# Making keys and values per node instead of per gathered edge row in a four-layer graph network

## The reference

```python
K = (x @ Wk.T + bk).reshape(N, HEADS, HEAD_DIM)
V = (x @ Wv.T + bv).reshape(N, HEADS, HEAD_DIM)
Q = x.reshape(N, HEADS, HEAD_DIM)
scores = jnp.sum(K[src] * Q[dst], axis=-1) / np.sqrt(HEAD_DIM)
m = jax.ops.segment_max(scores, dst, num_segments=N)
e = jnp.exp(scores - m[dst])
attn = e / (jax.ops.segment_sum(e, dst, num_segments=N)[dst] + 1e-16)
out = jax.ops.segment_sum(V[src] * attn[:, :, None], dst, num_segments=N)
return out.reshape(N, DIM_H) @ Wo.T + bo
```

## Time and profile before

| | |
|---|---|
| median of 3 runs | 6019.27 us (6014.14 to 6030.68) |
| the profiled execution | 6022.17 us |
| its span in the trace | 6020.4 us |
| its mean granted clock of TensorE | 0.809 of 2.4 GHz |
| busy, share of the span | PE 63%, DVE 66%, ACT 34%, POOL 50% |
| moved from and to HBM | 995 MB, 165 GB/s |

### The profile page before, as it was taken

The page is one execution under the profiler, slowest core; times in us unless marked ns, Lnnn a source line. Parts: engine busy times, 40 slices in busy tenths (PEclk is TensorE's granted clock), DMA queues, the critical chain, the costliest instruction groups (busy, mean ns, idle before and its releaser), DMA issues. The chain is left out here.

```text
span 6020.4 us, 90405 instructions
## 1 busy us (share of the span) xinstructions
PE 3782.8 (63%) x16668; PEld 2549.2 (42%) x16668; DVE 3973.2 (66%) x12622; ACT 2020.3 (34%) x4450; POOL 2987.1 (50%) x2764
## 2 busy tenths in 40 slices
PE   0688884333489985559965556776500198988940
PEld 0466653333267764444444445555400043433410
DVE  8555555888388873654455556656578798888856
ACT  0444452333122221225556542222144433333310
POOL 0644442777677600000057768777700267777730
PEclk9788886555799997989977779888855599999975
DMA  6566665777455544877777767777578511111149
GB/s 226 147 160 159 156 159 152 230 221 211 121 127 145 142 157 153 255 241 229 229 230 234 226 187 135 133 127 133 94 256 271 177 32 38 43 46 47 48 156 377
DMA packets 986437, 994.99 MB, mean 165 GB/s; under 512 B 210641, under 2 KB 648417, under 8 KB 986163
## 3 DMA queue, kind: packets, MB, share of 16 engines
q1 hardware_dynamic: 676899, 628.12, 36.1%
q0 software_dynamic: 131904, 146.31, 12.7%
q10 hardware_dynamic: 177488, 218.95, 10.3%
HBM read 560.95 MB, written 466.16 MB: 171 GB/s over the span
## 5 line engine op out<-in xcount | busy, mean ns | idle before, releaser
L703 POOL DMA_INDIRECT at_first_table<-n_h,n_first_edge x784 | 792.6, 1011 | 1280.9 <-ACT n_h L271 924.5
L2489 PE MATMUL e_m<-e_by_rel,rel_w 128*128 128x512 f32 x1568 | 727.9, 619 | 0.0
L695 POOL DMA_INDIRECT e_xs<-x_table,e_idx x392 | 376.8, 961 | 514.1 <-POOLq L2379 395.0
L695 POOL DMA_INDIRECT e_x<-x,e_idx x392 | 376.9, 961 | 447.5 <-ACT e_h L271 241.0
L695 POOL DMA_INDIRECT e_hs<-h_table,e_idx x392 | 422.3, 1077 | 172.1 <-issue 108.1
L2403 DVE SCALAR_TENSOR_TENSOR e_by_rel<-e_y,e_part_t 128x512 f32<-128x512 f32 x784 | 476.5, 681 | 33.3 <-PE e_y L2504 27.7
L703 POOL DMA_INDIRECT rel_sum_table<-e_res,e_again x392 | 393.8, 1005 | 148.8 <-issue 125.5
L2489 PEld LDWEIGHTS e_m<-e_by_rel,rel_w 128*128 128x128 f32 x1568 | 306.1, 201 | 352.8 <-issue 352.8
L1008 PE MATMUL n_m<-n_mean,n_pick 128*128 128x129 f32 x784 | 203.4, 440 | 338.7 <-DVE n_pick L1073 323.0
L2481 PE MATMUL e_t<-ident,e_part 128*128 128x128 f32 x392 | 69.1, 304 | 550.7 <-ACT e_part L271 438.7
L711 POOL DMA_INDIRECT sum_table<-e_res,e_target x196 | 308.5, 1574 | 139.5 <-issue 58.9
(11 more groups left out here) (374 smaller groups left out, 10328.1 us busy)
## 6 DMA issues: line engine op xcount, KB each, us to landing
x_table<-n_x ACTq DMA_DIRECT2D x294, 256.0 KB
n_x<-x_table SPq DMA_DIRECT2D x294, 256.0 KB
e_hd<-at_first_table SPq DMA_DIRECT2D x196, 256.0 KB
mean_runs_table<-e_packed SPq DMA_DIRECT2D x196, 130.0 KB
n_mean<-mean_runs_table SPq DMA_DIRECT2D x392, 65.0 KB
at_first_table<-prep_zero ACTq DMA_DIRECT2D x1, 25088.0 KB
e_edge<-edge128T SPq DMA_DIRECT2D x98, 256.0 KB
e_keep<-col_tab_table SPq DMA_DIRECT2D x196, 128.0 KB
```

The source lines that it names most:

```text
L695: pool.indirect_dma_start(out=tile[:, t, :], out_offset=None, in_=table, in_offset=bass.IndirectOffsetOnAxis(ap=idx[:, col + t:col + t + 1 ...
L703: pool.indirect_dma_start(out=table, out_offset=bass.IndirectOffsetOnAxis(ap=idx[:, t:t + 1], axis=0), in_=tile[:, t, :], in_offset=None, ...
L2489: ins = pe.matmul(flat(at(ps_m, u - 6)), k.rel_w[:, r, :], at(by_rel, u - 6)[:, r, :], start=(r == 0), stop=(r == RELS - 1))
```

## The change

Each node's 128 keys and 128 values (without their biases) are made in the mean node stage and stored side by side as one row of 1 KB in a new table `key_val`. There PE turns the four tiles of `h1` (four transposes), ACT copies them from PSUM to `h1t`, PE multiplies each with `wkv`, the two weight matrices side by side (four products of 256 columns), ACT copies these in two halves to `key_val` and issues the store. ACT's list grows from a lag of 5 turns to one of 10, PE's from 1 to 8. `h1` is still stored and scattered.

The edge stage gathers from `key_val`. PE turns the key half alone, DVE multiplies it straight from PSUM with the queries (the keys' bias is added there, as before) one turn earlier than before, and ACT copies the value half, from SBUF, into a ring of 30 in place of `hst`. The key product and the value product are gone from PE's list, and DVE's message product reads the copied values in SBUF. The freed PSUM banks make both turning targets double. The gather of a slot now waits for PE's turning and for ACT's copy.

```diff
@@ mean node stage, PE
+                j = i - 8
+                if live(j, S):
+                    pe.wait_ge(h1t_ready, j + 1)
+                    if begun(j - 1):
+                        pe.wait_ge(key_val_ready, j)
+                    for t in range(TILES):
+                        ins = pe.matmul(ps_kv[t // HALVES][:, t % HALVES, :], at(h1t, u)[:, t, :], k.wkv[:, :], start=True,
+                                        stop=True)
+                    ins.then_inc(key_val_done, 1)
+                j = i - 6
+                if live(j, S):
+                    pe.wait_ge(h1_ready, j + 1)
+                    if begun(j - 1):
+                        pe.wait_ge(h1t_ready, j)
+                    for t in range(TILES):
+                        ins = pe.transpose(ps_h[:, t, :], at(h1, u - 6)[:, t, :], k.ident[:, :])
+                    ins.then_inc(h1_turned, 1)
@@ mean node stage, ACT
+                        act.wait_ge(h1_turned, j - 3)
                     norm.apply(act, at(h1, u), at(x1, u), ACT.Relu, j, u).then_inc(h1_ready, 1)
...
+                j = i - 7
+                if live(j, S):
+                    act.wait_ge(h1_turned, j + 1)
+                    if begun(j - 2):
+                        act.wait_ge(key_val_done, j - 1)
+                    act.activation(at(h1t, u - 7)[:, :, :], ps_h[:, :, :], ACT.Copy).then_inc(h1t_ready, 1)
+                j = i - 9
+                if live(j, S):
+                    act.wait_ge(key_val_done, j + 1)
+                    if begun(j - 4):
+                        act.wait_ge(at(key_val_out, u - 9), moved(j - 4, u - 9))
+                    for b in range(HALVES):
+                        ins = act.activation(at(key_val, u - 9)[:, HALVES * b:HALVES * b + HALVES, :], ps_kv[b][:, :, :],
+                                             ACT.Copy)
+                    ins.then_inc(key_val_ready, 1)
+                j = i - 10
+                if live(j, S):
+                    act.wait_ge(key_val_ready, j + 1)
+                    act.dma_start(rows_of(scratch["key_val"], j), flat(at(key_val, u - 10))
+                                  ).then_inc(at(key_val_out, u - 10), 16)
+            run_steps(act, body, S, 10, 16)
@@ edge stage
-        hs, hs_in = ph.loaded("hs", [P, TILES, D])
+        hs, hs_in = ph.loaded("hs", [P, TILES, 2 * D])
-        hst, hst_ready = ph.made("hst", [D, ROWS], HELD)
+        val, val_ready = ph.made("val", [P, TILES, D], HELD)
-        ps_hs, ps_hd, ps_k, ps_v, ps_p, ps_r = (ph.ps(n) for n in ("hs", "hd", "k", "v", "p", "r"))
+        ps_hs, ps_hd, ps_p, ps_r = ph.banks("kt"), ph.banks("qt"), ph.ps("p"), ph.ps("r")
@@ edge stage, POOL
                     pool.wait_ge(hs_turned, i - 3)
+                    pool.wait_ge(val_ready, i - 3)
                 pool.sem_inc(pool_turn, 1)
-                gather(pool, at(hs, i), scratch["h1"], idx[:, i, :], 0, at(hs_in, i))
+                gather(pool, at(hs, i), scratch["key_val"], idx[:, i, :], 0, at(hs_in, i))
@@ edge stage, DVE
-                j = n - 3
+                j = n - 2
                 if 0 <= j < S:
-                    dve.wait_ge(k_done, j + 1)
+                    dve.wait_ge(hs_turned, j + 1)
...
-                    dve.scalar_tensor_tensor(at(kq, j)[:, :], flat(ps_k), k.bk[:, :], at(hdt, j)[:, :], ALU.add, ALU.mult
+                    dve.scalar_tensor_tensor(at(kq, j)[:, :], flat(at(ps_hs, j)), k.bk[:, :], at(hdt, j)[:, :], ALU.add, ALU.mult
...
-                                      ps_v[:, :, :].rearrange("p t (h c) -> p t h c", c=HEAD_DIM),
+                                      at(val, j)[:, :, :].rearrange("p t (h c) -> p t h c", c=HEAD_DIM),
@@ edge stage, ACT
-                    act.wait_ge(hs_turned, j + 1)
+                    act.wait_ge(at(hs_in, j), moved(j, j, TILES))
                     if j >= HELD:
-                        act.wait_ge(v_done, j - HELD + 1)
-                    act.activation(at(hst, j)[:, :], flat(ps_hs), ACT.Copy).then_inc(hst_ready, 1)
+                        act.wait_ge(pv_ready, j - HELD + 1)
+                    act.activation(at(val, j)[:, :, :], at(hs, j)[:, :, D:2 * D], ACT.Copy).then_inc(val_ready, 1)
@@ edge stage, PE
-                    if i:
-                        pe.wait_ge(hst_ready, i)
+                    if i >= 2:
+                        pe.wait_ge(kq_ready, i - 1)
                     for t in range(TILES):
-                        ins = pe.transpose(ps_hs[:, t, :], at(hs, i)[:, t, :], k.ident[:, :])
+                        ins = pe.transpose(at(ps_hs, i)[:, t, :], at(hs, i)[:, t, 0:D], k.ident[:, :])
                     ins.then_inc(hs_turned, 1)
-                j = n - 2
-                if 0 <= j < S:
-                    pe.wait_ge(hst_ready, j + 1)
-                    if j:
-                        pe.wait_ge(kq_ready, j)
-                    pe.matmul(flat(ps_k), k.wk[:, :], at(hst, j)[:, :], start=True, stop=True).then_inc(k_done, 1)
...
-                j = n - 29
-                if 0 <= j < S:
-                    pe.wait_ge(hst_ready, j + 1)
-                    if j:
-                        pe.wait_ge(pv_ready, j)
-                    for t in range(TILES):
-                        ins = pe.matmul(ps_v[:, t, :], at(hst, j)[:, t * P:(t + 1) * P], k.wv[:, :], start=True, stop=True)
-                    ins.then_inc(v_done, 1)
```

More of the change, by code:

```diff
@@ L285, in __init__ @@
         self.w1_edge = tile("w1_edge", [D, D])
-        self.wk = tile("wk", [D, D])
-        self.wv = tile("wv", [D, D])
+        self.wkv = tile("wkv", [D, 2 * D])
         self.wo = tile("wo", [D, D])
@@ L438, in _ @@
                 (w2, a["L0_W2"]),
-                (k.wk, a["L1_WkT"]), (k.wv, a["L1_WvT"]), (k.wo, a["L1_WoT"]), (k.w_node, a["L2_W_node"]),
+                (k.wkv[:, 0:D], a["L1_WkT"]), (k.wkv[:, D:2 * D], a["L1_WvT"]), (k.wo, a["L1_WoT"]), (k.w_node, a["L2_W_node"]),
                 (w_center_t, a["L2_W_centerT"]), (w_cat_node, a["L2_W_cat"][0:D, :]),
@@ L959, in mean_nodes @@
         h1, h1_ready = ph.made("h1", [P, TILES, D], 4)
-        x1_out, h1_out = ph.dma_sems("x1_out"), ph.dma_sems("h1_out")
+        h1t, h1t_ready = ph.made("h1t", [D, TILES, P])
+        key_val, key_val_ready = ph.made("key_val", [P, TILES, 2 * D], 4)
+        x1_out, h1_out, key_val_out = ph.dma_sems("x1_out"), ph.dma_sems("h1_out"), ph.dma_sems("key_val_out")
+        h1_turned, key_val_done = ph.sem("h1_turned"), ph.sem("key_val_done")
         kept_ready, mean_done, copy_turn = ph.sem("kept_ready"), ph.sem("mean_done"), ph.sem("copy_turn")
@@ L964, in mean_nodes @@
         ps_m = [[ph.ps(f"m{u}{b}", (P, HALVES, D + 1)) for b in range(HALVES)] for u in range(2)]
+        ps_h = ph.ps("h")
+        ps_kv = [ph.ps(f"kv{b}", (P, HALVES, 2 * D)) for b in range(HALVES)]
         block = ph.ctx.enter_context(nc.Block())
@@ L1010, in body @@
                     ins.then_inc(mean_done, 1)
-            run_steps(pe, body, S, 1)
+                j = i - 8
[15 more added lines that the diff above has]
+                    ins.then_inc(h1_turned, 1)
+            run_steps(pe, body, S, 8, 12)
         @block.vector
@@ L1099, in body @@
                     act.dma_start(rows_of(scratch["h1"], j), flat(at(h1, u - 5))).then_inc(at(h1_out, u - 5), 16)
-            run_steps(act, body, S, 5, 12)
+                j = i - 7
[19 more added lines that the diff above has]
+            run_steps(act, body, S, 10, 16)
             for u in range(SLOTS):
+                act.wait_ge(key_val_out[u], all_moved(S, u))
                 act.wait_ge(x1_out[u], all_moved(S, u))
@@ L1136, in attention_edges @@
         pool_turn = ph.sem("pool_turn")
-        hs_turned, hd_turned, k_done, score_done = (ph.sem(n) for n in ("hs_turned", "hd_turned", "k_done", "score_done"))
-        v_done, pack_done, out_done, carry_done = (ph.sem(n) for n in ("v_done", "pack_done", "out_done", "carry_done"))
+        hs_turned, hd_turned, score_done = (ph.sem(n) for n in ("hs_turned", "hd_turned", "score_done"))
+        pack_done, out_done, carry_done = (ph.sem(n) for n in ("pack_done", "out_done", "carry_done"))
         head_win, consts_ready = ph.sb("head_win", [D, 2 * GH - HEADS]), ph.sem("consts_ready")
@@ L1403, in _ @@
                         dve.wait_ge(hdt_ready, j)
-                    dve.tensor_tensor_scan(at(hdt, j)[:, :], at(keep, j)[:, :], flat(ps_hd),
+                    dve.tensor_tensor_scan(at(hdt, j)[:, :], at(keep, j)[:, :], flat(at(ps_hd, j)),
                                            at(hdt, j - 1)[:, ROWS - 1:ROWS] if j else 0.0, ALU.mult, ALU.add
@@ L1409, in _ @@
                     g, t = divmod(j, GROUP)
-                    dve.wait_ge(v_done, j + 1)
+                    dve.wait_ge(val_ready, j + 1)
                     dve.wait_ge(weight_t_ready, g + 1)
@@ L2637 @@
     scratch["rel_sum"] = table("rel_sum", (R, D))
+    scratch["key_val"] = table("key_val", (R, 2 * D))
     scratch["tt"] = table("tt", (D, R))
```

7 lines of the change are left out of this document (3 added, 4 removed).

## The result

| | before | after |
|---|---|---|
| median (lowest to highest), us | 6021.39 (6014.14 to 6030.68), 4 runs | 6118.52 (6109.19 to 6125.96), 4 runs |
| span of the profiled execution, us | 6020.4 | 6110.1 |
| first index load of the edge stage to the next stage's first load | 1541.4 to 2383.7 = 842.3 | 1539.7 to 2478.7 = 939.0 |
| in it: first gather to last gather | 1545.3 to 2126.0 = 580.7 | 1543.7 to 2218.7 = 675.0 |

The kernel after takes 1.0163 times as long, 95% interval 1.0146 to 1.0181: 97 us more, outside the predicted range. I cut both spans at the same DMA issues first. The edge stage lost 96.7 us, the whole of it, and 94.3 of that lie between its first and its last gather. The mean node stage, where the work went, ends 1.7 us earlier than before. So in these two traces the work that was added cost nothing, and the stage that was relieved of work became slower.

What follows compares the result with a forecast made beforehand. PE was taken to bound the middle of the edge stage at 6.60 us a step, POOL the mean node stage. Terms -27 + 10 + 4 = -13 us gave 6009, as a median 6006; range 5986 to 6065.

Steps and rivals of the forecast that it cites:

- Rival 2: Edge stage: 1 KB rows stretch each gather; at +0.3 us per gather +68 us, 6087; chance 0.13.
- rival 3: Edge stage does not gain, since SP's stores or uneven softmax steps hold it at 6.5 us; 6026; chance 0.15.
- floor for SP: Edge stage, middle: SP's own chain, less its waiting for DVE, allows a step of 5.9 us.
- 0.40 us a step: Edge stage, 68 middle steps: gain from a lighter PE, 27 us, of at most 0.49 a step or 33 us.
- DVE's floor: Edge stage, middle: step of 6.11 us, 6.60 less 0.49 of waiting for PE; DVE is late next.
- collision on POOL: Edge stage: message product with two SBUF inputs delays gathers by 0.5 us in half the steps; POOL's floor 5.66 to 5.9.
- 14 us that I took: Mean node stage: cost of the added work, 10 us for DMA load and 4 us for the drain.
- loop 4.3 us: Mean node stage: new round of PE products and ACT copies at full clock, below POOL's 5.34 us, so at nothing.
- DMA +10: Mean node stage: the 512 KB store per step adds DMA load, taken as +0.1 us a step, 10 us.
- drain +4: End of mean node stage: ACT's lag grows from 5 to 10 steps; about +4 us, 20 without POOL's lag.
- rival 1: Mean node stage pays more through clock or DMA: step 5.7 us, 35 us, plus drain 18; 6045; chance 0.22.
- last 36 steps: End of edge stage: SP repeats every 6.37 us, its stores waiting for one another; the change leaves it at 6.4.

## Why the prediction was wrong

**The step that failed** is the one not priced. I counted "PE drops below DVE (6.11), SP (5.9) and POOL (5.66), so DVE is late next. Its work is unchanged in count", and took no wait for the key product, which the change moves from n-3 to n-2. Each engine's work was right, but the floor of a step was not among engines: it was the round of 7.9 us that the ring of two closes. The diff shows the moved index; the `score_done` wait below it stayed as it was, and stands in the kernel. I followed the value forward (who waits for the key product) and not back (what it waits for, and where that stands in PE's order). None of my rivals had it. Rival 2, at 6087, came nearest in size by another mechanism, which the runs exclude: gathers at 0.954 us in the first steps, not 1.24. What shows the round: two edits of the changed kernel that open it (80 and 83 us back), one edit of the kernel before that closes it (99 us lost), and the rings of two and three buffers compared with the stores apart (94.9 us).

**The next step down is rival 3.** With the round open, SP's pair of stores holds the edge stage at 852.1 us on the first chip and 840.7 on the third, where the trace of the kernel before has 842.3; the whole kernel is 15 and 6 us slower than before. As the rival said, gathers of twice the bytes make the landings longer. My floor for SP, 5.9 us, was read at a DMA share of 0.55; at 0.68 the step is 350/53 = 6.6. I gave this rival 0.15.

**The size of the gain came near once both were out of the way, in part by luck:** 0.40 us a step forecast, 6.60 - 6.25 = 0.35 measured, and 27 us forecast against 23. DVE's floor was about right: (350 - 10.0)/56 = 6.07, forecast 6.11. POOL's was not: I allowed 5.9, and it is 6.13, above DVE's. Which of the two holds a given step was not tested; POOL is the one that never pauses.

**The collision on POOL** is there, and larger than priced once the step is short. The gather at 1957.57, just behind the start of the message product that now reads SBUF twice, took 1.34 us, where its neighbours take 0.95. Counted over the timelines from 1750 to 2100 us: of the gathers begun while a message product ran, none of 29 took over 0.95 us in the kernel before, where the product reads PSUM and SBUF, and 26 of 28 took 1.24 to 1.48 us in the kernel after. Each of the 26 is longer by what the product still had to run, less about 0.13 us. With the stores apart only 4 of 35 are stretched so, since most begin when the product is nearly done; other operations of DVE stretch gathers too, as they did before (1.137 against 0.944). The mean over these 350 us is 1.156 us in the kernel after, 1.148 and 1.200 with the third buffer, and 1.232 with the stores apart. The Trainium skill (SBUF — State Buffer, "Who interferes with whom") has the second instruction blocked until the first is done. Begun 0.53 us before that product ended, the gather took 0.39 us more, and so with the others: the trace agrees with the rule. In the kernel after no step was lost to it, since POOL waited for its slots anyway; with the stores apart it is part of POOL's 6.13 us.

**The mean node stage cost less than the 14 us that I took.** Forecast: clock 0.87, loop 4.3 us, DMA +10, drain +4. The trace has 0.86 for the clock from 1350 to 1400 us and 0.92 from 1050 to 1500; the stage ends no later, with scatters unchanged. DMA carries 315 GB/s at a share of 0.96 at no cost to POOL. Measured alone it is 9 us, with an interval from 1 to 19; within the changed kernel the stage runs from 976.5 to 1539.7 us (last store of the stage before to first index load of the edge stage), 563.2 long, against 979.3 to 1541.4, 562.1. The Trainium skill (DMA: Bandwidth & Descriptors, "Where 436 GB/s comes from") gives one core 358 GB/s, under which this load fits; the trace agrees as far as this stage goes, while the 382 GB/s of the last stage lie above that figure. The low cost holds for two of the three chips. On the slow one the edge stage starts 40 to 50 us later with the node part, a size near rival 1's 35 + 18; what differs on that chip was not settled.

**The last 36 steps** were unchanged, as said. SP's period in the kernel after:

```profile
2336.16 2.37 SPq L1275 DMA_DIRECT2D att_runs_table<-e_packed  x2
...
2342.52 2.38 SPq L1275 DMA_DIRECT2D att_runs_table<-e_packed  x2
```

6.36 us, against 6.37. The first 30 steps too: 80 gathers in 100 us, 5.0 us a step. Of the last part I had read that the stores wait for one another, and put no price on it. Nearly all of the 42 us of the moved store lie there: from last gather to the stage's end 257.7 us before, 216.7 with the stores apart.

## What to carry to other kernels

- When a producer moves one turn earlier, count its ring backwards: with R buffers, step j waits for the consumer of step j - R. Find the turn and the place in the consumer's list where that stands. If it is the same turn, behind something that waits for the producer's own engine, the turn becomes serial. A third buffer was worth 83 us here, and 95 with the stores apart.
- All engines at 60 to 75% with a steady step can be the sign of such a round; here it was. An "issue" wait that comes back every step may be a semaphore: look in the timeline for what ended just before, here 0.1 us.
- Transfers that wait for one another go apart in the queue, with the other transfers between them. Price them at the DMA share that the change will bring, not at today's.
- Before calling one engine the limit, look for another that never pauses. Here DVE was at 93% and POOL, with its 0.30 us between gathers, at all of its time.

## What the runs showed that I had not expected

- An indirect gather of 128 rows takes POOL the same time at 512 B and at 1 KB a row (0.944 and 0.954 us in the first steps), with the DMA share at 0.52 and 0.62.
- A DMA share of 0.96 to 0.97, kept up through the mean node stage, slowed neither its scatters nor the engines that feed them on two chips. Yet SP's waits for single stores in the edge stage grew from 1.78 to 2.38 us between shares of 0.57 and 0.68. Throughput was free, latency was not.
- A lighter PE can have a lower granted clock: 0.94 in the middle with the third buffer, where PE was busy 287 of 350 us, against 1.00 at 345. Busy time alone does not order it: the kernel after has 0.97 at 242, and the kernel before with the stricter wait 1.00 at 312.
- One of the three chips of the experiments ran every kernel 11% slower, and gave another answer on the node part (40 to 50 us later, in place of 0 to 9). Totals are only comparable on one chip.
